# A transformer decoder layer in fp32: both attentions and the middle of batch 0 in one common order

## Chip, cores and metric

One core of one Trainium2 chip. The metric is the device time of one execution in microseconds. Every kernel is run several times; where two are compared, they ran on the same chip.

## The reference

Input `x` is (2, 1024, 256), `ctx` is (2, 77, 256), all in fp32, with 16 heads of 16 channels.

```python
xn1 = ln(x, g1, be1)
sa = mha(xn1, xn1, Wq_s, Wk_s, Wv_s, causal=True)
x = x + (sa @ W1 + b1)
xn2 = ln(x, g2, be2)
ca = mha(xn2, ctx, Wq_c, Wk_c, Wv_c, causal=False)
x = x + (ca @ W2 + b2)
xn3 = ln(x, g3, be3)
return x + relu(xn3 @ Wf1 + bf1) @ Wf2 + bf2
```

In `mha` the scores are q.k divided by `D ** -0.5` (that is, multiplied by 4), then softmax over the keys, then the product with v. All projections have biases.

## The kernel before

**Tiles and groups.** The 2 x 1024 rows are four chunks of 512 (`NCH`, two per batch). The 32 pairs of batch and head are 8 groups (`NG`) of four heads; groups 0 to 3 are batch 0, 4 to 7 batch 1. Queries and keys are split into three bf16 parts; the six products of parts that matter are stacked on the rows of the contraction (`QP`, `KP`, 96 rows), so that a score is one bf16 matmul. Splitting is done by `split` units: ScalarE takes the first part out of PSUM (`first_part`, L804), VectorE forms the rest (L1225), ScalarE the second part (`second_part`, L811), GpSimd the third (`third_parts`, L648), and SyncE stores all three to DRAM (L461). From there they are loaded as stacks (`load_stacks`, L482).

**An attention group.** TensorE forms q.k tiles ("chunks", L1029, with a mask product L1033 on the diagonal) in a ring of three PSUM banks; VectorE takes their row maxima (L1262). When a group's last maximum is there, GpSimd splits the negated maxima into three bf16 parts (L682 to L691), TensorE turns them (L1040), VectorE copies them to `shift_t` (L1275), and SyncE writes them with three DMAs (L503) as three more rows of the query stack. `shift_t` is one buffer, so the next copy waits for that transfer to land. Then the scores (k.q plus shift, 99 rows, L1066) go to three other banks ("units": 44 in a self group, 8 in a cross group), and ScalarE writes their exponentials (L832) to `probs`. GpSimd zeroes above the diagonal (`mask`, L699). The products with v (L1096) add into two banks of `out_region`, columns 0 to 511 and 512 to 1023; a causal group works in six steps of key tiles, [0], [1], [2], [3], [4,5], [6,7]. ScalarE copies a group's output (`copy_out`, L843), SyncE packs the sums (L428) and heads (L436); every second group VectorE inverts the sums (L1291), SyncE stores (L511) and spreads them (L521), and VectorE divides the heads (L1301).

**What orders the work.** `Attention.order` (L139) makes one list per attention: for every group its score units and products, and, placed among them by a running cost, the uses of the three-bank ring: chunks (ahead by `lead`), shift, and late in batch 1 the row products (`rows`, L1051) of chunks 0 and 1 with their norm. All five engines walk this list. `product_at` places each bank piece of a step alone: the one half way through the next step's scores, the other at its end. `moves` places packing, inversion, storing, spreading and division by group and unit. Each attention has its own semaphores, and its uses are counted from zero.

**Between the attentions** the order is written out by hand for each engine. TensorE (from L1127): the self list to its end, `turn_norm` (L928) of chunks 0 and 1, their query projections `qc` (L958, two units of one 512-column product each), then, when the self heads 4 to 7 are divided, `heads_product` (L974) of chunks 2 and 3, turn and projection of chunk 2, the first 12 items of the cross list, turn of 3, four items, projection of 3, the rest. SyncE (L574 ff.) stores the parts of each chunk and loads stacks of cross groups 0 and 1 after chunk 1, 2 and 3 after chunk 2, 4 when all is stored; groups 5 to 7 are loaded in pieces within the cross list. Row products of the second output (`rows` with W2) of chunks 0 and 1 lie in the last cross group (L1051). The feed-forward follows (L1183, L974).

Of the kernel before, what the change touches and what calls it, by code (L numbers as in the profile page):

```python
# [19 lines left out]
ALU = mybir.AluOpType  # L20
ACT = mybir.ActivationFunctionType
AX = mybir.AxisListType
# [43 lines left out]
class Attention:  # L66
# [8 lines left out]
    def __init__(self, causal, keys, buffers, lead, gap, rows):  # L75
        self.causal, self.keys, self.nb = causal, keys, buffers
# [19 lines left out]
        self.pieces = []  # L96
        for ui, (tiles, _) in enumerate(self.steps):
            if len(tiles) == 1:
                self.pieces += [(ui, [(0, bank)]) for bank in ((1, 0) if causal else (0, 1))]
            elif ui + 1 < self.n_steps:  # L100
                self.pieces += [(ui, [(n, 1)]) for n in range(len(tiles))]
            else:
                self.pieces.append((ui, [(n, 1) for n in range(len(tiles))]))
        self.n_pieces = len(self.pieces)

        if causal:
            first = [self.first_unit(ui) for ui in range(self.n_steps + 1)]
            self.product_at = {}
            for n, (ui, _) in enumerate(self.pieces):
                to = (ui + 1) % self.n_steps  # L110
                half, end = (first[to] + first[to + 1]) // 2, first[to + 1] - 1
                alone = sum(p[0] == ui for p in self.pieces) == 1
                late = n > 0 and self.pieces[n - 1][0] == ui or alone
                self.product_at.setdefault(end if late and not alone else half, []).append((ui + 1 == self.n_steps, n))
        else:
            self.product_at = {2 * GH - 1: [(0, 0)], GH - 1: [(1, 1)]}
# [13 lines left out]
        if causal:  # L130
            ends = [max(u for u, (ui, _, _) in enumerate(self.units) if ui == step) for step in (1, 1, 1, 3)]
            self.moves = dict(zip(("inverted", "stored", "spread", "divided"), ((1, u) for u in ends)))
            self.moves["packed"] = (1, 2 * GH)
        else:
            self.moves = {"packed": (2, 1), "inverted": (2, 5), "stored": (2, 5), "spread": (2, 7), "divided": (3, 6)}
        self.load_at = list(range(2 * len(Q_RUNS))) if causal else list(range(0, 2 * len(Q_RUNS), 2))
        self.order(lead, gap, rows)

    def order(self, lead, gap, rows):  # L139

        def spread(costs):
            total, at, out = sum(costs), 0.0, []
            for c in costs:
                out.append(at / total)
                at += c
            return out  # L150
        unit_at = spread([self.unit_width(u) + BANK for u in range(len(self.units))])
        chunk_at = spread([nh * w + 64 for _, _, nh, _, w in self.chunks])
        stream = [(g + chunk_at[c], ("chunk", g, c)) for g in range(NG) for c in range(len(self.chunks))]
        stream += [(g + 1 + gap, ("shift", g)) for g in range(NG)]
        for n, (first, second, normed) in enumerate(rows):
            stream += [(first + lead, ("rows", n, 0)), (second + lead, ("rows", n, 1)), (normed + lead, ("norm", n))]
        stream.sort(key=lambda e: e[0])
        self.pe, self.uses = [], []

        def use(what):  # L160
            if what[0] == "norm":
                self.pe.append(what)
                return
            self.pe.append(("m", len(self.uses)))
            self.uses.append(what)

        for g in range(NG):
            for u, (ui, h, k) in enumerate(self.units):
                while stream and stream[0][0] <= g + unit_at[u] + lead:
                    use(stream.pop(0)[1])  # L170
                self.pe.append(("score", g, u))
                for lag, n in self.product_at.get(u, []):
                    if g >= lag:
                        self.pe.append(("product", g - lag, n))
        for _, what in stream:
            use(what)
        self.pe.append(("product", NG - 1, self.n_pieces - 1))
        self.use_at = {what: i for i, what in enumerate(self.uses)}
# [5 lines left out]
    def pieces_to(self, step):  # L184

        g, ui = divmod(step, self.n_steps)
        return self.n_pieces * g + sum(p[0] <= ui for p in self.pieces)

# [4 lines left out]
    def unit_index(self, g, ui):  # L193

        return g * len(self.units) + self.first_unit(ui)

    def behind(self, what, g, u):

        lag, unit = self.moves[what]
        return g - lag if g >= lag and u == unit else None  # L200

    def left(self, what):

        return range(NG - self.moves[what][0], NG)

    def step_end(self, g, u):

# [10 lines left out]

ACT_NORMS = [0, 1, 2, 3, 2 * NCH, 2 * NCH + 1]
SELF_EARLY = [14, 18, 22, 26, 30, 36, 44]

CROSS_EARLY = [12, 16]
# [1219 lines left out]
```

## Time and profile before

| | us |
|---|---|
| median of 3 runs | 598.66 (596.15 to 600.23) |
| the profiled execution | 595.19 |
| its span, first to last instruction | 593.3 |
| TensorE, VectorE, ScalarE, GpSimd busy | 492.2, 334.3, 322.1, 189.5 |
| mean granted TensorE clock | 0.945 |

The profile is of one execution. PE is TensorE's matmuls, PEld its weight loads, DVE VectorE, ACT ScalarE, POOL GpSimd, SP or SPq SyncE and its DMA queue. L12 is line 12 of the kernel. A row of a timeline gives start, duration, engine, line, output<-input and how many instructions are merged; in brackets is how long the engine was idle before and what released it. The x of matmuls of fp32 data counts two records each.

### The profile page before, as it was taken

What the parts mean: (1) busy time and instruction counts of PE and PEld (TensorE: products, weight loads), DVE (VectorE), ACT (ScalarE), POOL (GpSimd) and SP (SyncE); (2) the same over time, 40 slices, a digit from 0 to 9 for tenths busy, and PEclk for the clock granted to TensorE, in tenths of its full rate; (3) what the DMA queues carried; (4) which work ended last, traced back from release to release, by engine and by line L of the source; (5) the groups of instructions that cost most, each with busy time, mean ns of one, the idle gap of its engine ahead of it and who ended that gap; (6) DMA issues with size and microseconds to landing.
All of it is one profiled execution on the core that took longest, in us unless ns stands there. A gap on an engine that the chain in (4) does not pass through costs nothing.

```text
span 593.3 us, 8855 instructions
## 1 busy us (share of the span) xinstructions
PE 492.2 (83%) x3296; PEld 281.7 (47%) x3296; DVE 334.3 (56%) x645; ACT 322.1 (54%) x622; POOL 189.5 (32%) x291
## 2 busy tenths in 40 slices
PE   1588974999999999999998867867786577999887
PEld 1485641343434343434343235432323366988877
DVE  3165985877778777787841225654541466263340
ACT  3685311767676767676766750245673753344360
POOL 2497970121212121213131352423323273030200
PEclk9998997999999999999998998778887978999999
DMA  8145945025261616160205037376733310101001
GB/s 278 60 130 180 222 129 104 1 40 89 43 112 43 98 34 115 31 114 9 68 19 161 0 95 175 91 160 114 115 76 76 75 39 0 36 2 36 19 19 35
DMA packets 31082, 48.11 MB, mean 81 GB/s; under 512 B 8832, under 2 KB 25728, under 8 KB 28928
## 3 DMA queue, kind: packets, MB, share of 16 engines
q1 hardware_dynamic: 30904, 47.52, 34.9%
q8 instruction: 26, 0.43, 0.3%
q14 instruction: 16, 0.13, 0.1%
q10 hardware_dynamic: 136, 0.03, 0.1%
HBM read 30.66 MB, written 12.03 MB: 72 GB/s over the span
## 4 chain that ended last, share of the span: by engine, by line
PE 58%; DMA 15%; DVE 9%; ACT 8%; issue 3%; POOL 2%; SPq 2%; ACTq 0%; DVEq 0%
PE ps L974 12%; PE ps L1096 12%; PE ps L1066 10%; PE ps L1029 9%; PE ps L1183 8%; DMA stacks<-shift_t 5%; DMA sums<-out_t 4%; DVE max_a L1262 4%; DMA recips<-recip_rows 4%; PE ps L958 3%; ACT arena_p L832 3%; PE ps L1051 2%; PE ps L1033 2%; ACT out_t L843 2%; DMA recip_rows<-sums 1%
## 5 line engine op out<-in xcount | busy, mean ns | idle before, releaser
L832 ACT ACTIVATE arena_p<-ps 128x512 f32<-128x512 f32 (+4 forms) x416 | 194.6, 537 | 121.8 <-PE ps L1066 120.4
L1262 DVE TENSOR_REDUCE max_a<-ps 128x1 f32<-128x512 f32 (+4 forms) x280 | 161.9, 621 | 65.0 <-PE ps L1029 49.5
L1066 PE MATMUL ps<-stacks 99*128 99x512 bf16 (+1 forms) x448 | 140.5, 347 | 32.8 <-DMA stacks<-shift_t 24.9
L1029 PE MATMUL ps<-stacks 96*128 96x77 bf16 (+4 forms) x640 | 137.5, 287 | 11.7 <-DVE max_a L1262 8.2
L1096 PE MATMUL ps<-arena_p,v_group 128*32 128x512 f32 (+3 forms) x896 | 99.8, 524 | 1.6 <-POOL arena_p L699 1.2
L699 POOL TENSOR_SCALAR_AFFINE_SELECT arena_p<-arena_p 128x512 f32<-128x512 f32 x64 | 39.9, 635 | 177.4 <-ACT arena_p L832 177.4
L1029 PEld LDWEIGHTS ps<-stacks 96*128 96x128 bf16 x640 | 53.8, 103 | 87.9 <-DVE max_a L1262 48.5
L1066 PEld LDWEIGHTS ps<-stacks 99*128 99x128 bf16 x448 | 42.5, 100 | 92.0 <-ACT arena_p L832 46.2
L1262 DVE TENSOR_REDUCE max_b<-ps 128x1 f32<-128x384 f32 (+3 forms) x88 | 52.4, 634 | 6.7 <-PE ps L1033 6.6
L1242 DVE TENSOR_TENSOR xs<-ps,xs 128x512 f32<-128x512 f32 x24 | 16.4, 690 | 68.8 <-PE ps L974 45.7
L908 ACT ACTIVATE hid_r<-ps,col 128x512 fp32r<-128x512 f32 x32 | 22.0, 688 | 54.0 <-PE ps L1183 51.7
L974 PE MATMUL ps<-wf2r,hid_r 128*128 128x256 f32 x384 | 47.1, 284 | 4.9 <-DVE hid_r L1377 3.8
L639 POOL TENSOR_TENSOR xs<-xs,row 128x256 f32<-128x256 f32 x48 | 39.6, 860 | 33.3 <-DVE xn L1217 33.3
L1033 PE MATMUL ps<-maskb,identb 128*128 128x128 bf16 x256 | 50.1, 222 | 0.0
L974 PEld LDWEIGHTS ps<-wf2r,hid_r 128*128 128x128 f32 x384 | 46.4, 192 | 6.0 <-DVE hid_r L1377 4.5
L1183 PE MATMUL ps<-xn_r,wf_high 128*128 128x512 f32 x128 | 40.9, 402 | 8.4 <-DVE xn_r L1370 8.4
L1377 DVE TENSOR_TENSOR hid_r<-arena_p,hid_r 128x512 fp32r<-128x512 f32 x32 | 29.1, 925 | 21.6 <-ACT arena_p L911 21.5
L928 PE MATMUL ps<-identf,xn 128*128 128x128 f32 x96 | 16.6, 325 | 25.7 <-ACT xn L868 11.6
L648 POOL TENSOR_TENSOR parts<-arena_p,parts 128x512 bf16<-128x512 f32 (+1 forms) x26 | 29.2, 1150 | 24.2 <-ACT parts L811 24.1
L1225 DVE SCALAR_TENSOR_TENSOR arena_p<-ps,col,parts 128x512 f32<-128x512 f32 (+1 forms) x26 | 18.5, 719 | 28.9 <-ACT parts L804 28.9
L1096 PEld LDWEIGHTS ps<-arena_p,v_group 128*32 128x32 f32 x896 | 18.9, 109 | 29.0 <-issue 17.3
L804 ACT ACTIVATE parts<-ps,col 128x512 bf16<-128x512 f32 (+1 forms) x26 | 17.0, 663 | 28.8 <-PE ps L958 27.3
(73 smaller groups left out, 520.6 us busy)
## 6 DMA issues: line engine op xcount, KB each, us to landing
arena_h<-out_t SPq DMA_DIRECT2D x16, 256.0 KB, 5.3
recips<-recip_rows SPq DMA_DIRECT2D x8, 512.0 KB
q_parts<-parts SPq DMA_DIRECT2D x8, 384.0 KB, 2.7
k_parts<-parts SPq DMA_DIRECT2D x8, 384.0 KB, 2.9
qc_parts<-parts SPq DMA_DIRECT2D x8, 384.0 KB, 3.6
stacks<-qc_parts SPq DMA_DIRECT2D x8, 384.0 KB, 6.0
stacks<-q_parts SPq DMA_DIRECT2D x7, 384.0 KB, 4.9
stacks<-k_parts SPq DMA_DIRECT2D x7, 384.0 KB, 7.6
```

The lines of the kernel that those rows point to most:

```text
L639: ins = pool.tensor_tensor(xt, xt, row[:, r, :], ALU.add)
L648: pool.tensor_tensor(p[:, 2, :], rest[:, u % 4, 0:width], p[:, 1, :], ALU.subtract)\
L699: pool.affine_select(out=blk, in_=blk, compare_op=ALU.is_ge, fill=0.0, base=0, pattern=[[0, GH], [1, P]], channel_multiplier=-1).then_inc( ...
L832: nc.scalar.activation(probs[0:a.kp, a.probs_slot(g, ui), h, k * BANK:k * BANK + width], ps[0:a.kp, unit % S_BANKS, 0:width], ACT.Exp, sca ...
L974: ins = nc.tensor.matmul(acc[:, j, :], lhs_t(k, j), rhs(k), start=(k == 0), stop=(k == n_k - 1))
L1029: ins = nc.tensor.matmul(m_bank(use)[:, o:o + w], q_stack[0:ROWS, g % a.nb, h, t * P:(t + 1) * P], k_rows(ROWS, g, h, s0, s0 + w), start=T ...
L1033: ins = nc.tensor.matmul(m_bank(use)[:, o + w - P:o + w], identb[:, :], maskb[:, :], start=False, stop=True)
L1066: ins = nc.tensor.matmul(ps[:, unit % S_BANKS, lo - k * BANK:hi - k * BANK], k_rows(ROWS_S, g, h, i * P, (i + 1) * P) if a.causal else k_c ...
L1096: ins = nc.tensor.matmul(out_region[32 * h:32 * h + 32, lo:hi], v, probs[:, slot, h, o:o + hi - lo], start=(i == 0), stop=last, skip_group ...
L1183: ins = nc.tensor.matmul(ps[:, 2 + u % 4, :], wf1r[hw][:, kc, f * P:(f + 1) * P], xn_r[:, hx, k % 2, kc, :], start=(i == 0), stop=(i == le ...
L1262: nc.vector.tensor_reduce(dst, m_bank(use)[:, 0:nh * w].rearrange("p (h w) -> p h w", h=nh), AX.X, ALU.max).then_inc(s.max_read, 1)
L1377: nc.vector.tensor_tensor(hid_r[:, LO, f, :], full[:, (U_H + u) % 2, :], hid_r[:, HI, f, :], ALU.subtract).then_inc(hid_low, 1)
```

## The change

Both attentions, the middle of batch 0 and that of batch 1 become one list, `STREAM`, that all engines walk from the first self group to the last cross score. Events get a time on a common scale (26 us a self group, 6.5 us a cross group, `END` after the eighth self group), are sorted by it, and only their order is used.

- The two bank pieces of a causal step become one product run, at the end of the next step's scores.
- `rows` of chunks 0 and 1 move to groups 5.2 and 5.8; their norm's turn and query projections (`turn`, `qproj`) become uses of the three-bank ring, at groups 6.25 and 6.6. The row products, turns and projections of chunks 2 and 3 are uses too, 17 to 32 us after END. `xn_mid` and `rest_mid` are places of their own for them.
- Cross groups 0 to 3 start at END, groups 4 to 7 at END + 26 + `END_GAP` (32). Their maxima start 13 to 17 us earlier. The cross groups use stack slots 2, 0, 3, 1, 4.
- The stacks of cross groups 0 to 2 are loaded in self group 7, 3 just after END, and 4 to 7 together when all query parts are stored. The first feed-forward weight, 1 MB, is loaded just before them ("raw").
- The row products of the second output for chunks 0 and 1 move from the last cross group into the gap (END + 47 and + 51).
- The semaphores of scores, exponentials, products, maxima and ring uses are common to both attentions.

The core of the diff:

```diff
-        self.pieces = []
-        for ui, (tiles, _) in enumerate(self.steps):
-            if len(tiles) == 1:
-                self.pieces += [(ui, [(0, bank)]) for bank in ((1, 0) if causal else (0, 1))]
...
+            for ui, (tiles, _) in enumerate(self.steps):
+                self.pieces.append((ui, [(n, bank) for n, tile in enumerate(tiles)
+                                         for bank in range(tile[1] // BANK, 2)]))
+                to = (ui + 1) % self.n_steps
+                self.product_at[self.first_unit(to + 1) - 1] = (ui + 1 == self.n_steps, ui)
...
+SELF_US, CROSS_US = 26.0, 6.5
+END = NG * SELF_US
+def order():
+    events = []
+    starts = [g * SELF_US for g in range(NG)]
+    SELF.place(events, starts, SELF_US, [t - 1.35 * SELF_US for t in starts], [t - 0.23 * SELF_US for t in starts])
+    crossed = [END + CROSS_US * g + (END_GAP if g >= NG // B else 0.0) for g in range(NG)]
+    leads = [17.0, 17.0, 15.0, 13.0, 13.0, 14.0, 15.0, 16.0]
+    CROSS.place(events, crossed, CROSS_US, [t - a for t, a in zip(crossed, leads)],
+                [t - a + CROSS_US + 1.8 for t, a in zip(crossed, leads)])
...
+        if g % 2 and g < NG - 3:
+            add(nxt + 1.6 * CROSS_US, "inverted", CROSS, g)
+            add(nxt + 1.62 * CROSS_US, "stored", CROSS, g)
+            add(nxt + 1.64 * CROSS_US, "spread", CROSS, g)
+            add(nxt + 2.9 * CROSS_US, "divided", CROSS, g)
...
+    for n, t in enumerate([5.2 * SELF_US, 5.8 * SELF_US, END + 17.0, END + 20.0]):
+        for half in range(2):
+            add(t + 1.5 * half, "rows", SELF, n, half)
+        add(t + 6.0, "norm", SELF, n)
+    for n, t in enumerate([6.25 * SELF_US, 6.6 * SELF_US, END + 24.5, END + 28.0]):
+        for kc in range(KC):
+            add(t + 0.4 * kc, "turn", SELF, n, kc)
+        for hh in range(2):
+            add(t + 3.0 + 1.0 * hh, "qproj", SELF, n, hh)
+            add(t + 5.0 + 1.0 * hh, "second", SELF, n, hh)
+    for n, t in enumerate([END + 9.0, END + 13.0, END + 33.0, END + 37.0]):
+        add(t, "bias", SELF, n)
+    for g, t in enumerate([7.1 * SELF_US, 7.15 * SELF_US, 7.2 * SELF_US, END + 0.5]):
+        add(t, "load", CROSS, g)
+    for g in range(NG // B, NG):
+        add(END + 35.5 + 0.1 * g, "load", CROSS, g)
+    w2 = END + 47.0
+    for n in range(2):
+        for half in range(2):
+            add(w2 + 4.0 * n + 1.5 * half, "rows", CROSS, n, half)
+        add(w2 + 8.0 + 4.0 * n, "norm", CROSS, n)
+    add(END + 34.5, "raw", SELF, 0)
...
+                    elif op == "load":
+                        wait_parts(U_QC + NCH if what[0] < NG // B else U_H)
+                        load_stacks(a, *what)
+                    elif op == "raw":
+                        sp.wait_ge(split_p, U_H)
                         sp.dma_start(wf1, w_f1.rearrange("(k p) n -> p k n", p=P)).then_inc(ff_in, 16)
...
+            def bank_free(use):
+
+                if use < M_BANKS:
+                    return
+                held = RING[use - M_BANKS]
+                if held[0] == "turn":
+                    pe.wait_ge(tp_read, 2 * (NCH + held[2]) + held[3] + 1)
+                else:
+                    pe.wait_ge(use_read, dve_uses(use - M_BANKS))
```

## Rows read from the trace of the kernel before

**Rows 1.** PE busy share by stretch; us, then busy and (instructions) of each engine, clock, DMA share, GB/s

```profile
162.00:221.00 59.00, 56.39 (x441) 23.02 (x440) 46.55 (x81) 40.67 (x89) 13.42 (x28) 1.00 0.40 70
...
310.00:340.00 30.00, 26.40 (x169) 9.23 (x168) 6.72 (x24) 20.76 (x46) 7.50 (x12) 0.94 0.27 80
...
358.00:396.00 38.00, 27.59 (x147) 17.93 (x146) 21.01 (x54) 8.15 (x12) 12.03 (x22) 0.77 0.63 139
...
396.00:466.00 70.00, 54.19 (x401) 24.55 (x399) 30.52 (x77) 40.80 (x79) 20.65 (x44) 0.85 0.47 89
...
381.00:389.00 8.00, 7.47 (x45) 4.77 (x42) 4.47 (x12) 2.24 (x3) 2.95 (x8) 0.79 1.06 217
```

**Rows 2.** TensorE's timeline, group 4: start, us, engine, line, tiles; two products, what follows each

```profile
227.74 1.07 PE L1096 MATMUL ps<-arena_p,v_group 128*32 128x512 f32 x8
...
228.74 0.39 PE L1029 MATMUL ps<-stacks 96*128 96x512 bf16 x1
...
247.09 0.43 PE L1096 MATMUL ps<-arena_p,v_group 128*32 128x128 f32 x8
...
247.45 0.39 PE L1029 MATMUL ps<-stacks 96*128 96x512 bf16 x1
```

**Rows 3.** groups of instructions, 162 to 222 us: busy us, mean ns, idle before

```profile
L832 ACT ACTIVATE arena_p<-ps 128x512 f32<-128x512 f32 (+1 forms) x89 | 40.9, 528 | 18.3 <-PE ps L1066 18.2
```

**Rows 4.** TensorE's timeline from the last self groups to the last cross score

```profile
302.21 1.89 PE L1051 MATMUL ps<-wmid,arena_h 128*128 128x256 f32 x8
...
339.07 0.34 PE L1066 MATMUL ps<-stacks 99*128 99x256 bf16 x2
...
342.16 1.09 PE L928 MATMUL ps<-identf,xn 128*128 128x128 f32 x8
...
346.63 7.21 PE L958 MATMUL ps<-arena_p,wmid 128*128 128x512 f32 x16
...
385.47 3.76 PE L958 MATMUL ps<-arena_p,wmid 128*128 128x512 f32 x8
...
464.48 0.60 PE L1066 MATMUL ps<-stacks 99*128 99x512 bf16 x2
```

**Rows 5.** the chain of waits, 340 to 480 us: start, us, what

```profile
343.34 4.04 DMA sums<-out_t
...
348.08 1.46 DMA recip_rows<-sums
...
349.56 6.66 DMA recips<-recip_rows
...
386.55 8.72 DMA stacks<-shift_t
...
399.77 5.18 DMA stacks<-shift_t
...
424.57 3.82 DMA recip_rows<-sums
```

**Rows 6.** SyncE's DMA issues in the same stretch

```profile
380.99 3.67 SPq L482 DMA_DIRECT2D stacks<-qc_parts  x6
...
396.69 1.83 SPq L482 DMA_DIRECT2D stacks<-qc_parts  x3
```

**Rows 7.** groups of instructions, 340 to 396 us

```profile
L1262 DVE TENSOR_REDUCE max_a<-ps 128x4 f32<-128x308 f32 x19 | 7.9, 471 | 1.8 <-PE ps L1029 1.8
...
L794 ACT ACTIVATE arena_p<-ps,col 128x512 f32<-128x512 f32 x8 | 6.0, 775 | 19.5 <-PE ps L928 17.9 <-issue 1.3
...
L1205 DVE BATCH_NORM_STATS2 stats<-xs 128x6 f32<-128x256 f32 x8 | 2.8, 413 | 0.1
...
L1242 DVE TENSOR_TENSOR xs<-ps,xs 128x512 f32<-128x512 f32 x4 | 2.7, 687 | 4.8 <-PE ps L974 4.8
...
L639 POOL TENSOR_TENSOR xs<-xs,row 128x256 f32<-128x256 f32 x8 | 5.5, 732 | 0.0
...
L1301 DVE TENSOR_TENSOR arena_h<-arena_h,recips 128x1024 f32<-128x1024 f32 x1 | 1.2, 1224 | 0.9 <-DMA recips<-recip_rows 0.9
```

More of the change, by code:

```diff
@@ L94, in __init__ @@
             self.units = [(0, h, k) for k in range(T // BANK) for h in range(GH)]
-        self.pieces = []
-        for ui, (tiles, _) in enumerate(self.steps):
-            if len(tiles) == 1:
-                self.pieces += [(ui, [(0, bank)]) for bank in ((1, 0) if causal else (0, 1))]
[L100 to L103, printed above, removed]
-        self.n_pieces = len(self.pieces)
[L106 to L116, printed above, removed]
+        self.pieces, self.product_at = [], {}
+        if causal:
+            for ui, (tiles, _) in enumerate(self.steps):
[4 more added lines that the diff above has]
+        else:
+            self.pieces = [(0, [(0, bank)]) for bank in range(2)]
+        self.n_pieces = len(self.pieces)
         self.n_copies = 1 if causal else 2
@@ L136, in __init__ @@
[L136 to L178, printed above, removed]
@@ L191, in unit_width, with units_to, pieces_to @@
         return min(BANK, self.steps[ui][1] - k * BANK)
[L193 to L204, printed above, removed]
+    def units_to(self, g, ui=0):
+        return self.unit0 + g * len(self.units) + self.first_unit(ui)
+    def pieces_to(self, g, n=0):
+        return self.piece0 + g * self.n_pieces + n
     def step_end(self, g, u):
@@ L213, in probs_slot, with slot_free @@
         return (self.n_steps * g + ui + (not self.causal)) % P_SLOTS
-SELF = Attention(True, T, buffers=3, lead=1.35, gap=0.12, rows=[(6.8, 6.9, 7.15), (7.3, 7.4, 7.6)])
-CROSS = Attention(False, S_CTX, buffers=5, lead=2.3, gap=0.5, rows=[(7.05, 7.15, 7.55), (7.6, 7.7, 7.99)])
+    def slot_free(self, g, ui):
+        step = self.n_steps * g + ui - P_SLOTS
+        if step >= 0:
+            return self.pieces_to(step // self.n_steps, sum(p[0] <= step % self.n_steps for p in self.pieces))
+        if not self.before:
+            return 0
+        b = self.before
+        last = max(n for n in range(NG * b.n_steps) if n % P_SLOTS == self.probs_slot(g, ui))
+        return b.pieces_to(last // b.n_steps, sum(p[0] <= last % b.n_steps for p in b.pieces))
@@ new lines, in spread, with place @@
+    def spread(self, costs):
+        total, at, out = sum(costs), 0.0, []
+        for c in costs:
+            out.append(at / total)
+            at += c
+        return out
+    def place(self, events, starts, length, chunk_starts, shifts):
+        unit_at = self.spread([self.unit_width(u) + BANK for u in range(len(self.units))])
+        chunk_at = self.spread([nh * w + 64 for _, _, nh, _, w in self.chunks])
+        for g in range(NG):
+            for c in range(len(self.chunks)):
+                events.append((chunk_starts[g] + length * chunk_at[c], 0, ("chunk", self, g, c)))
+            events.append((shifts[g], 0, ("shift", self, g)))
+            for u in range(len(self.units)):
+                t = starts[g] + length * unit_at[u]
+                events.append((t, 1, ("score", self, g, u)))
+                if u in self.product_at:
+                    lag, n = self.product_at[u]
+                    if g >= lag:
+                        events.append((t, 2, ("product", self, g - lag, n)))
@@ L221, with dve_uses @@
+END_GAP = 32.0
+STREAM, RING = order()
+USE_AT = {what: i for i, what in enumerate(RING)}
+def dve_uses(use):
+    return sum(what[0] != "turn" for what in RING[:use + 1])
 ACT_NORMS = [0, 1, 2, 3, 2 * NCH, 2 * NCH + 1]
-SELF_EARLY = [14, 18, 22, 26, 30, 36, 44]
-CROSS_EARLY = [12, 16]
 def at_least(eng, sem, value):
@@ new lines, in mask, with attention @@
+            def mask(g, ui):
+                pool.wait_ge(exps, SELF.units_to(g, ui + 1))
+                for i, q0, w, off in SELF.steps[ui][0]:
+                    blk = probs[:, SELF.probs_slot(g, ui), :, off:off + P]
+                    pool.affine_select(out=blk, in_=blk, compare_op=ALU.is_ge, fill=0.0, base=0,
+                                       pattern=[[0, GH], [1, P]], channel_multiplier=-1).then_inc(S1.masked, 1)
+            def attention():
+                set_v(0)
+                for op, a, *what in STREAM:
+                    if op == "use" and what[1][0] == "chunk" and what[1][3] + 1 == len(a.chunks):
+                        split_shift(a, what[1][2])
+                        if not a.causal and what[1][2] == NG - 1:
```

870 lines of the change are left out of this document (439 added, 431 removed).

## The prediction, made before the result was known

> **What bounds the kernel now.** First the busy share by stretch. In the steady self groups TensorE is busy 56.4 of 59 us, two groups of 29.5 us [rows 1]: it sets the pace, with ScalarE at 40.7 and VectorE at 46.6. In the last group (310 to 340) TensorE is still 26.4 of 30 busy, though no self maxima are left to form. Then it changes: 358 to 396 has 27.6 of 38 at clock 0.77, 396 to 466 has 54.2 of 70 at 0.85 [rows 1]. A clock of 0.77 is a mixture of the two levels, 2.4 and 1.2 GHz. The chain of waits says why: after the last self product it goes sums out (4.04), reciprocals stored (1.46) and spread (6.66), and later shift rows (8.72, 5.18) [rows 5]. So the middle is bound by a chain of small steps and transfers. I call END the end of the last self score, 339.07 + 0.34 = 339.4; the last cross score ends at 465.1 [rows 4], 125.7 us later. That distance and the length of the self groups are what the change touches. What follows the last cross score (a turn, copies, sums out, feed-forward) has the same instructions, and I leave it as it is.
>
> **Self groups, products joined.** The two bank pieces of a tile step become one run, 11 runs a group become 6. From the start of a 512-column piece to the next score or chunk are 1.00 us, from a 128-column one 0.36 [rows 2]. Linear in columns: 0.213 us per 128, so 0.15 us stay as a fixed price of a run. Five fewer runs save 0.75 us a group; with about as much again in gaps ahead of a run (227.74 is 0.1 us after its predecessor by the same view) up to 1.2. I take 1.0, 8 us over 8 groups. Against it: a run is now up to 2.0 us while three score banks hold three exponentials, 40.9/89 = 0.46 us each [rows 3], 1.4 us. ScalarE falls idle 0.6 us or so in five places a group; it has 18.3 us of idle in 60 [rows 3], so it costs nothing while TensorE is the bound. If that cover fails the price is 5 x 0.6 = 3 us a group. Bounds -10 to +8 us (two or three groups uncovered), taken -8.
>
> **Self groups, work moved in.** The eight row products of batch 0 (two of them per chunk and half, 1.89 us a half [rows 4]) only go from groups 6 and 7 to group 5: four halves, nothing in the sum. New in group 6 are two turns of 1.09 and four projections, 7.21 us together [rows 4]: 9.4 us. Until now these lay beside the recips transfer, in the shade of the chain, so none of the 9.4 us is won back there. Cross maxima of groups 0, 1 and part of 2 (19 uses) fall into group 7: between 2 us and 19 x 0.471 = 9 [rows 7]; I take 3, as TensorE writes such a use far faster than VectorE reads it. Each of 12 row, turn and projection uses now holds one of the three shared banks until a busy ScalarE or VectorE has read it (0.775, 0.687 [rows 7]); queued behind the blocked use on TensorE are all scores. Bounds 0 and 12 x 0.6 = 7, taken 2. VectorE in group 5 also gets sums and normalisation of two chunks, about 10 us on its 23 of 29.5, still under TensorE's 36.
> Self groups in sum: -8 + 9.4 + 3 + 2 = +6 us (END at about 345.5); bounds -3 to +15.
>
> **After END: the chain of batch 1.** Cross groups 0 to 3 need only batch 0, so their scores start near END instead of at 395, and fill the wait. But the end is set by batch 1. Times from END:
> Masks, last product and copy +5 (before 3.9: 343.34 is where the copy had ended; now four cross exponentials stand ahead of it). Sums out 4.0 to 5.3, reciprocal 0.6, store 1.46, spread 6.66, division 1.22 [rows 5, 7]: +20.5.
> Four halves of row products with one product run and a few scores between them, 4 x 1.75 + 2.3: +30. VectorE's queue has the second chunk's rows and statistics ahead of the first chunk's normalisation: 0.69 + 4 x 0.41 + 0.4, then 1.6: +34. Turn 1.1, two copies 1.6, and then projection, turn, projection, product run, two projections, 1.8 each and 1.1 and 1.0: +46. (Before, the last projection ended at 389.23 [rows 4], +49.8: the chain itself is hardly shorter, since it is the same chain.)
> From that end to the first load behind all stores it was 389.23 to 396.69, 7.5 us [rows 4, 6]. GpSimd's queue now has the bias of chunk 2 (4 x 0.73 [rows 7]) ahead of the last third part, some 1.7 of its 2.9 us show: +55.
> Then what I think decides. SyncE's list has, in this order: the 1 MB weight load, twelve loads for groups 4 to 7 (0.61 us an issue, 3.67 for six [rows 6]), and only then the store and the spread of the reciprocals of cross groups 2 and 3. VectorE's list has the division of those heads just ahead of the first maximum of group 4. So group 4 waits for the spread, not for its own operands. Twelve issues 7.3, store 3.8 (the value under load [rows 5]; 1.46 when quiet), spread 6.66, division 1.22: the division ends at +74.
> Division to first score of group 4: VectorE does eight maxima of group 4, four of group 5 (0.471), four row additions (0.687) and two sets of statistics (2.0), 12.5 us; waits for row products, first cold (3.4 by their doubled form), add 4; three shift issues and landing 6.9 (between 5.18 and 8.72 plus the issues [rows 5]): 23.5, so +97.5. Groups 5 to 7 follow one shift transfer each, since one buffer holds the shift rows: 3 x 7.1, and 5.5 for the last scores: +124.5, against +125.7 before.
> So what batch 0 gains is given back in the gap: -1 us. Bounds -20 (next part) and +8.
>
> A rule of the Trainium skill speaks against the change here. The row first: a shift transfer of 24 KB issued right behind six stack loads took 8.72 us, a free one 5.18 [rows 5]; and in that stretch the DMA share was 1.06 at 217 GB/s [rows 1]. "DMA: Bandwidth & Descriptors" (Queues, rings and completion order) says that each DMA engine consumes one issuer's descriptors in ring order. The trace agrees. By that rule the store waits for all bytes of the loads; the sum would then be that of the second rival.
>
> **Sum.** Profiled execution 595.2 (span 593.3) + 6 - 1 = 600. The median of the runs shown, 598.66, is 3.5 above the profiled one, so the measured median should be about 603: 0.8% above before.
>
> **Rivals.**
> *The gap closes* (faster). The lists place group 4's first maximum 45 us after END, its loads at 36. If the batch-1 chain runs near that, or group 4 starts on its loads alone (+55, landing 6.9, maxima 3.8 with the shift chain 3.7 + 6.9, so +78 instead of +97.5), the last score is at +105: 603 - 19.5 = 584. For it: row products and norms of cross batch 0 also leave the last group, and TensorE is idle for 26 of the 108 us between 358 and 466 [rows 1]. Against it: three queues (SyncE, VectorE, GpSimd) have the batch-0 leftovers in front.
> *The loads' bytes decide* (slower). Groups 4 to 7 load 4 x 768 KB = 3.1 MB (three runs of 384, 256 and 128 KB a group, by the sizes of the DMA issues). SyncE issues them in 7.3 us, but at the 217 GB/s of a saturated stretch [rows 1] they take 14.2; the store and spread behind them then land 7 us later, and everything after. It decides as soon as the queue moves less than 3.1 MB/7.3 us = 420 GB/s. With 4 us more of bank waits in groups 5 and 6: 603 + 7 + 4 = 614.
> *The order doesn't do what it says*: the cross scores of batch 0 don't start near END because group 0's shift rows come late (issued 8.7 planned us before, 5.2 to 8.7 in flight). Then groups 0 to 3 slide by up to 5 us, off the chain of batch 1: within 2 us of the forecast. It is part of its case.
>
> **How the numbers follow.** Forecast 0.40 (594 to 611 of its own), gap closes 0.32, bytes decide 0.28. A measurement of this kernel can tell 1% from no change, 592.7 and 604.6 here. The forecast's case gives 0.04 faster, 0.28 same, 0.08 slower; the gap case 0.29 faster, 0.03 same; the bytes case 0.28 slower. Together faster 0.33, same 0.31, slower 0.36. The range goes from just beyond the gap case's time on one side to just beyond the bytes case's on the other: 582 to 618.
>
> **What would show it.** In the changed profile: END near 345 (steady groups near 28.5 us; group 6 about 34); four cross groups scored by END + 33; the last projection near END + 46; VectorE's longest idle waiting for the recips transfer before the division of cross heads, while the stack loads of group 4 landed over 10 us earlier; group 4's first score near END + 97. Wrong would be: steady groups at 30 or more (then joined products starve ScalarE), or a first score of group 4 before END + 85 (then the gap closes), or after END + 103 (then the bytes decide).

## The result, and the profile after

The changed kernel takes 617.5 us (median of 4 runs, 614.9 to 618.9), the kernel before 598.6 (4 runs) on the same chip: a ratio of 1.0303 [1.0264, 1.0342]. It is slower by 3%. The profiled execution is 618.9 us with a span of 616.9, against 593.3 before, so 23.6 us are to be found.

First the start times of the copy that ends each self group, since their distances are the lengths of the groups. ScalarE's timeline of the kernel before (start, us, engine, line; groups 0, 4, 5 and 7):

```profile
135.80 1.04 ACT L843 ACTIVATE out_t<-ps 128x1024 f32<-128x1024 f32 x1
...
256.26 1.04 ACT L843 ACTIVATE out_t<-ps 128x1024 f32<-128x1024 f32 x1
285.69 1.04 ACT L843 ACTIVATE out_t<-ps 128x1024 f32<-128x1024 f32 x1
...
342.28 1.03 ACT L843 ACTIVATE out_t<-ps 128x1024 f32<-128x1024 f32 x1 [2.35 <-PE ps L1096]
```

The same of the changed kernel (groups 0, 4, 5, 6, 7):

```profile
136.31 1.02 ACT L929 ACTIVATE out_t<-ps 128x1024 f32<-128x1024 f32 x1
...
252.22 1.02 ACT L929 ACTIVATE out_t<-ps 128x1024 f32<-128x1024 f32 x1
293.93 1.02 ACT L929 ACTIVATE out_t<-ps 128x1024 f32<-128x1024 f32 x1
332.27 1.02 ACT L929 ACTIVATE out_t<-ps 128x1024 f32<-128x1024 f32 x1
358.70 1.02 ACT L929 ACTIVATE out_t<-ps 128x1024 f32<-128x1024 f32 x1
```

Four steady groups take 115.9 instead of 120.5 us (29.0 and 30.1 each). Then groups 5 and 6 take 41.7 and 38.3, and the last 26.4; before, these three took 86.0 us together, now 106.5. The last self score ends (TensorE's timeline of the changed kernel, to compare with 339.07 of [rows 4]) at 354.45:

```profile
353.83 0.62 PE L1156 MATMUL ps<-stacks 99*128 99x256 bf16 x4
```

So END is 15.0 us later than before. From END on, the chain of waits of the changed kernel (start, us, what) shows batch 1 on its way:

```profile
365.35 2.96 DMA recip_rows<-sums
368.32 7.64 DMA recips<-recip_rows
...
377.36 3.75 PE ps L1125 x8
...
402.50 3.64 PE ps L1142 x8
...
412.95 2.79 DMA qc_parts<-parts
415.79 0.62 SPq L565
...
423.00 0.58 SPq L565
423.62 13.78 DMA recip_rows<-sums
437.42 6.89 DMA recips<-recip_rows
...
465.43 1.86 DMA stacks<-shift_t
467.34 0.61 PE ps L1156
```

The line to look at is 423.62. The same 32 KB store took 1.46 us in a quiet stretch and 3.82 in a loaded one before [rows 5]. Here it stands on SyncE behind twelve stack loads and takes 13.78 us. The windows of the changed kernel (columns as in [rows 1]) show a steady stretch, as full of TensorE as before, and then this one: VectorE and ScalarE do nothing in it, TensorE works 0.94 of 22 us, and the DMA share is 0.98.

```profile
162.00:221.00 59.00, 57.14 (x461) 24.90 (x463) 48.04 (x85) 41.52 (x93) 13.48 (x28) 1.00 0.41 78
...
415.00:437.00 22.00, 0.94 (x12) 0.79 (x12) 0.00 (x0) 0.00 (x0) 0.64 (x1) 0.50 0.98 194
```

VectorE stands idle for 31 us before the division of the cross heads, as the forecast said it would. The last cross score ends at 488.42, END + 134.0, against END + 125.7 before: 8.3 us. (The last one starts at 488.03 and takes 0.39 us.) With the 15.0 of END that is 23.3 of the 23.6. What follows the last score is as long as before (128.5 and 128.2 us).

### The profile page after: what moved, and what is told of

Same layout as the page of the kernel before. It is cut to its first block, busy times and chain, and to the rows that moved or that the text cites. A ratio compares the mean times of both kernels' runs of the same rounds, so it can differ in the third digit from the quotient of the medians.

```text
span 616.9 us, 8823 instructions
## 1 busy us (share of the span) xinstructions
PE 488.4 (79%) x3296; PEld 285.0 (46%) x3296; DVE 329.2 (53%) x645; ACT 316.9 (51%) x622; POOL 187.2 (30%) x291
## 4 chain that ended last, share of the span: by engine, by line
PE 58%; DVE 14%; ACT 9%; DMA 9%; issue 3%; POOL 3%; SPq 2%; ACTq 0%; DVEq 0%
PE ps L1186 11%; PE ps L1047 10%; PE ps L1156 9%; PE ps L1103 8%; PE ps L1267 8%; DVE max_a L1344 6%; PE ps L1125 4%; ACT arena_p L915 4%; DMA recip_rows<-sums 3%; PE ps L1033 2%; PE ps L1142 2%; DMA recips<-recip_rows 2%; DVE max_b L1344 2%; PE ps L1107 2%; ACT out_t L929 1%
## 5 line engine op out<-in xcount | busy, mean ns | idle before, releaser
L915 ACT ACTIVATE arena_p<-ps 128x512 f32<-128x512 f32 (+4 forms) x416 | 191.1, 542 | 121.1 <-PE ps L1156 119.9
L1344 DVE TENSOR_REDUCE max_a<-ps 128x1 f32<-128x512 f32 (+4 forms) x280 | 158.4, 618 | 57.1 <-PE ps L1103 45.1
L1186 PE MATMUL ps<-arena_p,v_group 128*32 128x512 f32 (+3 forms) x896 | 92.9, 527 | 0.3 <-POOL arena_p L780 0.3
L958 ACT ACTIVATE xn<-xs,neg_mean,rstd 128x256 f32<-128x256 f32 x24 | 12.4, 588 | 68.7 <-POOL neg_mean L710 67.3
L1125 PE MATMUL ps<-wmid,arena_h 128*128 128x256 f32 x96 | 28.1, 443 | 24.7 <-DVE max_a L1344 20.8
L1186 PEld LDWEIGHTS ps<-arena_p,v_group 128*32 128x32 f32 x896 | 22.6, 111 | 30.7 <-issue 25.9
L1125 PEld LDWEIGHTS ps<-wmid,arena_h 128*128 128x128 f32 x96 | 20.7, 223 | 29.7 <-DVE max_a L1344 21.2
L1380 DVE TENSOR_TENSOR arena_h<-arena_h,recips 128x1024 f32<-128x1024 f32 x8 | 10.3, 1290 | 44.5 <-DMA recips<-recip_rows 34.1
```

The costliest lines, as they stand in the source:

```text
L915: nc.scalar.activation(probs[0:a.kp, a.probs_slot(g, ui), h, k * BANK:k * BANK + width], ps[0:a.kp, unit % S_BANKS, 0:width], ACT.Exp, sca ...
L1125: ins = nc.tensor.matmul(m_bank(use)[:, j * C:(j + 1) * C], heads_out[:, KC * b + kc, t0 + j * P:t0 + (j + 1) * P], wmid[:, kc, w0:w0 + C] ...
L1186: ins = nc.tensor.matmul(out_region[32 * h:32 * h + 32, lo:hi], v, probs[:, slot, h, o:o + hi - lo], start=(i == 0), stop=last, skip_group ...
L1344: nc.vector.tensor_reduce(dst, m_bank(use)[:, 0:nh * w].rearrange("p (h w) -> p h w", h=nh), AX.X, ALU.max).then_inc(use_read, 1)
```

## Experiments

In the diffs, a number behind END or a group is a place in the planned order of the kernel, not a measured time. Kernels tried together share the runs of the kernel before; each ratio is to that kernel (595.3 to 597.8 us in the three sets). "The changed kernel" is the one of the change, ratio 1.0303. A difference in us to the changed kernel is one of medians from different sets. By the ratios it can come out otherwise by 1 to 4 us, so small gains are read from the start times in the traces, each of one execution.

### The store of the reciprocals ahead of the loads

```
-            add(nxt + 1.62 * CROSS_US, "stored", CROSS, g)
-            add(nxt + 1.64 * CROSS_US, "spread", CROSS, g)
+            add(nxt + (8.3 if g == 3 else 1.62 * CROSS_US), "stored", CROSS, g)
+            add(nxt + (8.4 if g == 3 else 1.64 * CROSS_US), "spread", CROSS, g)
```

> The changed kernel, with the store and the spread of the reciprocals of cross groups 2 and 3 ahead of the weight load and the twelve stack loads in SyncE's order. Theory (the division of those heads, and with it group 4, waits for bytes queued ahead of the store): the store lands in 1.5 to 2.5 us instead of 13.78, the division comes at about 423 instead of 445 us, the first stack of group 4 lands about 3 us later than before (427), and group 4's first score moves from 467 to about 449: 617.5 - 18 = 599 us. Rival (group 4 is bound by its own stack loads and the maxima behind them): the loads now queue behind 512 KB of spread, nothing is gained, 615 to 620 us.

Measured: 608.3 us, ratio 1.0182 [1.0138, 1.0227]: 9 us won (7 by the ratios), half of what was expected or less. Its chain of waits:

```profile
411.50 2.31 DMA recip_rows<-sums
...
417.01 15.17 DMA stacks<-qc_parts
...
432.31 0.43 PE ps L1103 x4
```

The store now lands in 2.31 us, so its 13.78 were time behind the loads. But what is behind is late in its turn: the three stack loads of group 4 now have the spread (512 KB) and the weight (1 MB) in front, and the last of them lands 17 us after the first was issued.

### The weight load behind the stack loads

```
-    add(END + 34.5, "raw", SELF, 0)
+    add(END + 37.0, "raw", SELF, 0)
```

> The changed kernel, with the 1 MB feed-forward weight load moved behind the stack loads, the store and the spread. Theory (bytes in the queue ahead of the store set its landing): the store still waits for 3.1 MB, but not for the megabyte: 13.78 us becomes about 9.5, the total 613.5 us. Rival (the number of issues, 12 x 0.65 us, sets it): the store's landing stays near 13 us and the time at 617.5 within 1.

Measured: 617.6 us, 1.0355 [1.0293, 1.0416]: nothing won. That is what the rival forecast, though it named the number of issues as the reason. From the first load to the landed store it is 20.9 us instead of 21.6, and the spread then takes 8.47 us instead of 6.89, as the weight now follows it. The DMA view of this run, from 412 to 434 us, has little but the loads and the small store in it:

```profile
DMA packets 743, 3.19 MB, mean 145 GB/s; under 512 B 347, under 2 KB 359, under 8 KB 359
...
recip_rows<-sums SPq DMA_DIRECT2D x1, 32.0 KB, 13.0
```

This window has idle DMA engines at both ends. While they were full, from 414 to 432 us, the mean was 175 GB/s (columns as in [rows 1]):

```profile
414.00:432.00 18.00, 0.94 (x12) 0.79 (x12) 0.00 (x0) 0.00 (x0) 0.00 (x0) 0.50 1.01 175
```

In the changed kernel the DMA view shows the weight passing among the loads, 4.26 MB between 415 and 437 us:

```profile
DMA packets 1044, 4.26 MB, mean 194 GB/s; under 512 B 368, under 2 KB 404, under 8 KB 660
```

So it is the stack loads that take the time, and not their issues: SyncE has issued all twelve at 420.4, and they keep the engines full until 432. They do it at a rate of their own, which the forecast needed and took as 217 GB/s. The weight had been issued 2.4 us ahead of the first load and landed at 419.5, before any of them. No run has fewer loads with the same bytes, so a price for each load beside that for its bytes is not ruled out.

### Both together

> The changed kernel, with the store and spread of cross groups 2 and 3 ahead of the stack loads as in the first of these kernels, and the 1 MB weight behind the loads as in the second. Theory (after the first edit the first stack of group 4 is what is late, landing 17 us after its issue because spread and weight, 1.5 MB, are ahead of it in the queue): without the megabyte it lands about 5 us earlier, group 4's first score at about 450 instead of 455 us, total 603. Rival (the stack loads take that long by themselves once all twelve are in flight, as 3.1 MB took 21 us before): no more than 1.5 us against 608.3.

Measured: 600.5 us (10 runs), 1.0052 [1.0022, 1.0083]. The two edits are worth 17 us together (15 by the ratios), where the first alone gave 9 and the second none: with the store ahead of the loads, group 4 waits for its own loads, and the weight in front of them costs time. The chain of waits:

```profile
412.59 2.31 DMA recip_rows<-sums
...
417.03 10.00 DMA stacks<-qc_parts
...
427.17 0.43 PE ps L1103 x4
...
447.52 1.86 DMA stacks<-shift_t
...
449.43 0.61 PE ps L1156
```

The last cross score of this run, from TensorE's timeline:

```profile
470.14 0.39 PE L1156 MATMUL ps<-stacks 99*128 99x512 bf16 x1 [0.28 <-ACT arena_p L915]
```

Group 4's first score is at 449.43 instead of 467.34, 17.9 us earlier; the span is 17.5 shorter (599.4). So nearly the whole of this gap reaches the end of the kernel. This settles the middle: the order of the transfers around the reciprocals is worth 17 of the 18.9 us by which the changed kernel is slower (15 of 18 by the ratios). It is not the only loss. END is still late here, at 353.7. From there to the end of the last cross score it is 116.8 us, 8.9 less than in the kernel before: that is what the common order gains after END once the queue is in order (the turns and projections of batch 0 no longer stand there), and the late END takes it back.

### The joined products alone, in the kernel before

```
+            if causal:
+                self.pieces.append((ui, [(n, bank) for n, tile in enumerate(tiles)
+                                         for bank in range(tile[1] // BANK, 2)]))
...
-                self.product_at.setdefault(end if late and not alone else half, []).append(...)
+                self.product_at.setdefault(end, []).append((ui + 1 == self.n_steps, n))
```

> The kernel before, with only the two bank pieces of each causal step joined to one product run at the end of the next step's scores. Theory (a run has a fixed price on TensorE, five fewer a group): steady groups 1.1 us shorter, 8 groups, 598.6 - 8 = 590.6 us. Rival (the longer run starves ScalarE and VectorE, or the shorter groups of the changed kernel come from the other order of chunks): 597 to 603 us.

Measured: 589.8 us (6 runs), 0.9841 [0.9791, 0.9892], 8.0 us less than the kernel before (the interval is 6.5 to 12.5): the forecast's -8 lies in it, and no other kernel here is as fast. ScalarE's timeline, groups 0, 4 and 7:

```profile
135.90 1.08 ACT L846 ACTIVATE out_t<-ps 128x1024 f32<-128x1024 f32 x1
...
249.72 1.08 ACT L846 ACTIVATE out_t<-ps 128x1024 f32<-128x1024 f32 x1
...
332.92 1.03 ACT L846 ACTIVATE out_t<-ps 128x1024 f32<-128x1024 f32 x1 [2.35 <-PE ps L1099]
```

A group takes 28.5 us, 1.7 less than before, so the longer runs did not cost what ScalarE's waits were feared to.

### The products apart again, in the changed kernel

```
-                self.pieces.append((ui, [(n, bank) for n, tile in enumerate(tiles)
-                                         for bank in range(tile[1] // BANK, 2)]))
+                runs = ([[(0, 1)], [(0, 0)]] if len(tiles) == 1 else
+                        [[(0, 1)], [(1, 1)]] if ui + 1 < self.n_steps else [[(0, 1), (1, 1)]])
+                for m, run in enumerate(runs):
+                    at = end if m else half
```

> The changed kernel, with the products of a causal step in two runs again, half way and at the end of the next step's scores, as in the kernel before. Theory (the joined run is a gain of its own, 1.1 us a group): 617.5 + 8 = 625 us. Rival (in the crowded groups 5 and 6 the long runs are what starves ScalarE, so that joining is worth less here): 618 to 621 us.

Measured: 613.8 us, 1.0313 [1.026, 1.036], no different from the changed kernel. This was a miss: what is worth 8 us in the order of before is worth nothing in the new one. ScalarE's timeline of this kernel, groups 0, 4, 5, 6, 7:

```profile
137.59 1.06 ACT L933 ACTIVATE out_t<-ps 128x1024 f32<-128x1024 f32 x1
...
257.02 1.06 ACT L933 ACTIVATE out_t<-ps 128x1024 f32<-128x1024 f32 x1
295.72 1.05 ACT L933 ACTIVATE out_t<-ps 128x1024 f32<-128x1024 f32 x1
334.34 1.06 ACT L933 ACTIVATE out_t<-ps 128x1024 f32<-128x1024 f32 x1
359.40 1.02 ACT L933 ACTIVATE out_t<-ps 128x1024 f32<-128x1024 f32 x1
```

The steady groups do get longer, 29.9 against 29.0. But group 5 gets shorter by 3.0 (38.7) and the last by 1.3. Behind END it is 4.3 us less to the last cross score as well: the first row products after the wait for the spread take 1.97 and not 3.75 us, and store and spread of the reciprocals 1.7 us less. Nothing shows that these come from the joined runs. TensorE's timeline of the changed kernel in group 5 shows what a long run meets there:

```profile
259.36 0.34 PE L1103 MATMUL ps<-stacks 96*128 96x384 bf16 x1 [1.66 <-DVE max_a L1344]
...
260.58 3.42 PE L1186 MATMUL ps<-arena_p,v_group 128*32 128x512 f32 x16
...
267.93 0.39 PE L1103 MATMUL ps<-stacks 96*128 96x512 bf16 x1 [1.15 <-DVE max_a L1344]
```

TensorE has waited 1.66 us for a bank that VectorE had still to read, and the joined run behind it takes 3.42 us where the same form takes 1.71 at 354.38: it runs at 1.2 GHz (the granted clock is 0.55 from 260.5 to 264). Over 252 to 294 the granted clock is 0.96 here, and 1.00 with the products apart, and with the uses further apart below. But the slow run does not always follow that wait. The kernel with the weight load behind the stack loads has the same order up to END and the same waits of 1.66 and 1.15 us, and there the clock stays at 1.00 over that window:

```profile
258.69 1.92 PE L1186 MATMUL ps<-arena_p,v_group 128*32 128x512 f32 x16
```

Its group 5 takes 40.1 us, where the changed kernel and the six others profiled with this order took 41.4 to 41.7. So 1.6 of the 41.7 go with the low clock, which comes in most executions and not in all. That the waits came from the moved-in work is read from the trace, where VectorE has the addition of a row product and the statistics of a chunk (256.2 to 258.7) ahead of the maxima; the next run tests it.

### The moved-in uses further apart

```
-            add(t + 1.5 * half, "rows", SELF, n, half)
+            add(t + (1.5 if n > 1 else 4.0) * half, "rows", SELF, n, half)
-            add(t + 0.4 * kc, "turn", SELF, n, kc)
+            add(t + (0.4 if n > 1 else 1.8) * kc, "turn", SELF, n, kc)
```

(and the projections and second parts of chunks 0 and 1 at 1.8 instead of 1.0.)

> The changed kernel, with the row uses of chunks 0 and 1 spaced 4.0 instead of 1.5 planned us, their turn halves 1.8 instead of 0.4, their projections 1.8 instead of 1.0. Theory (in groups 5 and 6 TensorE waits because bunched uses hold the three banks): group 5 (41.7 us) and 6 (38.4 us) lose 5 us together, total about 612.5. Rival (those groups are long because VectorE and ScalarE have more to do there than TensorE covers, wherever the uses stand): END and the total move by less than 1.5 us.

Measured: 613.0 us, 1.0257 [1.0213, 1.0301], 4.4 us less than the changed kernel by the medians and 2.7 by the ratios, whose intervals overlap; 612.5 was expected. The traces are clearer, END comes 4.2 us earlier (350.2). ScalarE's timeline, groups 4 to 7:

```profile
252.02 1.02 ACT L929 ACTIVATE out_t<-ps 128x1024 f32<-128x1024 f32 x1
290.76 1.02 ACT L929 ACTIVATE out_t<-ps 128x1024 f32<-128x1024 f32 x1
326.33 1.02 ACT L929 ACTIVATE out_t<-ps 128x1024 f32<-128x1024 f32 x1
354.47 1.02 ACT L929 ACTIVATE out_t<-ps 128x1024 f32<-128x1024 f32 x1
```

Groups 5 and 6 take 74.3 instead of 80.1 us, with the same instructions in them. Their windows, in the changed kernel and here:

```profile
252.22:332.27 80.05, 70.50 (x462) 30.62 (x460) 46.41 (x93) 48.28 (x103) 20.36 (x36) 0.98 0.23 56
252.02:326.33 74.31, 67.76 (x462) 30.59 (x460) 46.20 (x93) 48.16 (x104) 21.19 (x36) 1.00 0.23 55
```

TensorE's idle time went from 9.55 to 6.55 us and its busy time from 70.50 to 67.76. So of the 5.7 us only 3.0 are waits that the spacing took away. The other 2.7 are busy time, and the slow product run alone is 1.5 to 1.7 of them. In the last group 1.7 came back, where TensorE waits 1.70 us just until the stack loads of cross group 0 have landed (330.66).

### Batch 0's turns and projections half a group later

```
-[6.25 * SELF_US, 6.6 * SELF_US, END + 24.5, END + 28.0]
+[6.7 * SELF_US, 6.95 * SELF_US, END + 24.5, END + 28.0]
-[7.1 * SELF_US, 7.15 * SELF_US, 7.2 * SELF_US, END + 0.5]
+[7.25 * SELF_US, 7.3 * SELF_US, 7.35 * SELF_US, END + 0.5]
```

(the places of the turns and of the loads; the lead of the first cross maxima is cut to 12 to fit.)

> The changed kernel, with the turns and projections of chunks 0 and 1 moved from groups 6.25 and 6.6 to 6.7 and 6.95, where no self maxima are left, the cross loads to 7.25 and later, and the first cross maxima 12 us ahead of their scores. Theory (work moved into a group that TensorE bounds costs its own length, in the last group part of it lies under the exponentials): groups 6 and 7, 64.8 us now, get 4 to 5 us shorter together, total about 613. Rival (the last group is as full as the others): within 1.5 us, or slower through late cross operands of batch 0.

Measured: 621.9 us, 1.0448 [1.0407, 1.0489], 4.4 more than the changed kernel. Group 6 shrank from 38.3 to 34.2 us, and the last grew from 26.4 to 34.1. Of these 7.7 us, 4.8 are one wait of TensorE, from 336.0 to 340.8, for the stack loads of cross group 0, which land at 340.73; behind it stands a product run at the low clock. It is the second half of the rival, late cross operands. So this run does not show whether the last group would have covered the work if the stacks had come in time.

### Smaller steps on the chain, and several edits in one

```
-    w2 = END + 47.0
+    w2 = END + 53.6
...
-            add(w2 + 4.0 * n + 1.5 * half, "rows", CROSS, n, half)
+            add(w2 + 2.0 * n + 1.0 * half, "rows", CROSS, n, half)
```

> The changed kernel, with the four row products of the second output for chunks 0 and 1 placed 53.6 to 56.6 instead of 47 to 52.5 planned us after END, that is behind the shift of group 4 instead of ahead of it. Theory (they and their statistics stand between the division and the shift on TensorE and VectorE, 22 us to the first score of group 4): the shift leaves about 12 us earlier but the products still stand ahead of the first score, so that score comes 4 to 6 us earlier, total 612.5. Rival (all of it is needed before the score anyway): within 1.5 us of 617.5.

Measured: 616.4 us, 1.0309 [1.0261, 1.0356]: the rival by the time. The row products of cross batch 0 still stand ahead of the first score of group 4 on TensorE. In the trace that score does come 4.4 us earlier after END, as the theory said (END + 108.5), and 2.9 of it are left at the last cross score; the medians are too coarse to show them.

The bias of the last chunks:

```
-[END + 9.0, END + 13.0, END + 33.0, END + 37.0]
+[END + 9.0, END + 13.0, END + 34.2, END + 37.0]
```

> The changed kernel, with the bias addition of chunk 2 on GpSimd behind instead of ahead of the last third part of the query projections. Theory (the last store, and with it all stack loads, waits for its 2.7 us): last store and everything behind it 2.7 us earlier, total 614.8. Rival (the loads are bound by the queue from there on): no change.

Measured: 615.7 us, 1.0288 [1.0244, 1.0331], within the error of the changed kernel, and of the 614.8 expected, so the runs decide nothing. From the last projection to the first load it was 8.85 instead of 9.6 us: the bias was gone from the way, but the store then had the packs of a cross group (16 and 256 KB) just in front and landed after 4.22 us, not 2.8.

The two edits of the queue, the uses further apart, the rows and the bias in one kernel:

> The changed kernel with five edits together: uses of groups 5 and 6 further apart, reciprocals first, weight late, second-output rows behind the shift, bias later. Theory (each removes its own link of one chain, so they add): 617.5 - 4.5 - 14 - 5 - 2.7 = 591 us. Rival (another wait takes over, for instance the landing of group 4's first stack): 597 to 603 us.

Measured: 597.4 us (12 runs), 0.999 [0.9964, 1.0016]: no different from before, at the low end of the rival's 597 to 603. Against the changed kernel it is 20 us, of 24 that the single runs add up to and 26 that were expected, and that only brings it back to where it came from.

The two edits of the queue, and the rows of cross batch 0 later still:

```
-    w2 = END + 47.0
+    w2 = END + 64.8
```

> The changed kernel with reciprocals first and weight late (600.5 us so far), and the second-output rows of chunks 0 and 1 placed 64.8 to 70.3 planned us after END, among the scores of groups 5 and 6, instead of 47 to 52.5. Theory (moving them only behind the shift won nothing because they still stood ahead of group 4's first score on TensorE; among scores they lie under ScalarE's exponentials): group 4's first score comes 10 us earlier, the last four groups get 3 us longer, total 594. Rival (the shift transfers of groups 5 to 7 pace the end anyway, and the rows hold the banks that the maxima need): 599 to 602.

Measured: 605.4 us, 1.0183 [1.0134, 1.0231]: 1.3% above the kernel with the two edits of the queue (1.0052), from which it differs only in the place of the rows; 594 was expected. The edit did what it says: the first score of group 4 is at 441.28, 8 us earlier. But from the first to the last score it then takes 35.0 us, where it took 21.1. Its chain of waits shows a part of it:

```profile
457.77 1.84 POOL wf_high L736
...
459.68 4.54 POOL wf_low L738
...
464.84 1.01 POOL rstd L705
...
466.66 1.57 ACT xn L958 x3
```

The late norm stands on GpSimd behind 6.4 us of splitting the feed-forward weights, ScalarE waits for the norm at the head of its own queue, and the exponentials of the cross groups stand behind it. That is some 6 of the 14 us; the others are not broken down. A step was taken off the chain, and a queue that I had not looked at took its place.

The last kernel with the uses further apart and the bias later as well:

> The same as e9_rows_among_scores, with the uses of groups 5 and 6 further apart and the bias later. Theory: 4.5 and 1 us less than that kernel, 588 to 589 us, as fast as the kernel before with joined products alone (589.8). Rival: the gains don't add, 594 or more.

Measured: 601.2 us, 1.009 [1.005, 1.013]; 588 was expected. It has the same fault: 36.1 us from the first score (436.82) to the end of the last.

## Where the prediction was right and where it was wrong

The forecast was 603 us, no change that can be measured; its range of 582 to 618 holds 617.5 by half a microsecond, and the slowest of the four runs, 618.9, lies beyond it. That it holds at all is luck, as the part on the last groups shows. What happened is the second rival, whose 614 is 3.5 us short, and the test given for it, a first score of group 4 later than END + 103, came out at END + 112.9.

**Products joined, -8: right.** The joined runs alone gave -8.0 in the order of before. The steady groups of the changed kernel lost 1.1 us each, inside the 1.0 to 1.2 of the forecast, and 29.0 us stand against the 28.5 named; the cover by ScalarE held. What the step did not foresee is that 4.3 us are given back in groups 5 and 7, which are that much shorter with the products apart.

**Work moved in, +14 with END at 345.5: the term that was too small.** The 9.4 us of turns and projections are TensorE's own time (10.2 in this trace) and were not covered in group 6. The waits for banks, "bounds 0 and 7, taken 2", are the mis-sized term. Groups 5 and 6 were put at 36 and 34 and took 41.7 and 38.3, 10 us more; spreading the same uses out won back 5.7 of these, 3.0 of waiting and 2.7 of busy time. I had priced one use held for 0.6 us and nothing for the clock. The trace shows waits of 1.15 and 1.66 us, with statistics or a normalisation of 1.4 us ahead of the bank's reader on VectorE, and a product run at the low clock. END came at 354.45, 15.0 later than before. That is the upper bound given for the sum, but the bounds -3 and +15 do not follow from the terms: theirs add up to +1.4 and +33.4.

**The last projection at +46: 5.7 us short.** It ended at 406.1, END + 51.7. Store and spread of the reciprocals took 2.96 and 7.64 us, with shift rows and packs of the cross groups issued from 362 to 373 us, and not the quiet 1.46 and 6.66 (2.5 us); the first row products after the wait were cold, 3.75 and 2.36 us where the later halves took 1.73, so that the four halves took 12.4 us and not 9.5 (3 us).

**From the projection to the first load, 9 us: right** (9.6). The bias of chunk 2, two third parts and a store are in the chain as listed.

**Loads and store, 7.3 + 3.8: the step that failed.** It is the sentence "Twelve issues 7.3, store 3.8 (the value under load)". From the first load to the landed store it was 21.6 us. The loads hold the queue until they have moved and not until they are issued, and the small store behind them lands 0.2 us after the last of them (437.23 and 437.40). The Trainium skill's rule from "DMA: Bandwidth & Descriptors" (Queues, rings and completion order), that an engine consumes its descriptors in ring order, agrees: the same store took 13.78 us behind the loads and 2.31 ahead of them. The rival had the mechanism but 217 GB/s, from 8 us that began with a burst; at the 175 GB/s of the loads alone 3.1 MB are 18 us, and the start and the landing of the first and last transfers make it 21. The kernel before had the price: from 364 to 371 us the first six loads of cross stacks moved 167 GB/s at a DMA share of 0.95. I gave it 0.28 with both of its facts in hand, a saturated share of 1.06 and 8.72 us for a shift transfer behind six loads [rows 1, 5]; a 3.8 us taken from another stretch should not have stood for a store behind 3.1 MB.

**Spread and division: right** (6.89 and 1.23; the division ended at END + 91.1 instead of + 74).

**Division to first score, 23.5: right** (21.8). **The last groups, 27: too much.** They took 21.1 us; a shift transfer lands in 1.86 us when no loads are in flight, and not in the 5.2 to 8.7 of [rows 5]. The forecast called the one of 5.18 us "a free one", but three stack loads had been issued just ahead of it [rows 6]. These 6 us hid a part of the larger error. With the last groups as long as forecast, the kernel would have taken 623 us, beyond the range: that is the luck.

**The gap closes (0.32): did not.** Its condition, group 4 starting on its loads alone, did not hold in the changed kernel. With both edits of the queue it does: the first chunk of group 4 waits for its landed stack (427.17). The last cross score then comes at END + 116.8, not at the + 105 of this rival, since the row products of cross batch 0 still stand in front and the stack lands at END + 73.3 and not at + 62, and with the late END the kernel ends at the time of before. That the order does less than it says did not matter: four cross groups were scored while batch 1 waited, though by END + 40.6 and not by + 33.

In sum, of the 23.6 us between the two spans: the steady groups -4.6, groups 5 to 7 +20.5 (9.4 of it the moved-in work itself), +8.3 from END to the last score, and -0.6 in small differences. With the two edits of the queue the third term is -8.9. These questions stay open. With the uses spread, groups 5 and 6 still take 74.3 us and not the 70 of the forecast; what the rest of it is was not separated. And the late norm with the splitting of the feed-forward weights behind it was not tried, and neither was the move of the turns to the last group with the cross stacks in time, so nothing here says that the new order could not beat 589.8.

## What to carry to other kernels

A small transfer that something waits for must be issued ahead of large ones that nothing waits for yet; price what stands behind large loads by their bytes at a rate measured on loads of that form, and not by the issue time. Work moved off a chain into a stage that its engine bounds can cost its full length there, and more where its result needs a shared bank that a busy engine empties. The gain on the chain must be larger than that. Here the chain lost 8.3 us as first ordered and gained 8.9 with the queue put in order, against 20.5 us in groups 5 to 7. Take the separable part first: the joined runs without the new order were the faster kernel.

## What was not expected of the hardware

Twelve loads of 384, 256 and 128 KB into the stacks, in flight from one queue, moved 175 GB/s while the DMA engines were full (share 1.01 from 414 to 432 us, the run with the weight late). With the plain 1 MB weight load in the same queue the changed kernel moved 343 GB/s from 415 to 419 us and 170 from 419 to 436. A 384 KB load landed after 10.1 us there (median of four), against 6.9 us (of two) in the kernel before, between 381 and 389 us. A store of 32 KB took 13.8 us behind the twelve and 2.3 in front. And in the middle of a stage that otherwise has the full clock, where TensorE waited for a bank for 1.66 us at most, a product run went at half of it (3.42 us instead of 1.71 for 16 instructions). The same order of instructions ran at the full clock in another execution, so two traces of one stage can differ by 1.6 us for this alone.
